# Delta-rule attention beside a mixture of experts: keys turned by VectorE and a staged copy, copies shared out anew

## What is computed

```
# gated delta rule, 16 key heads, 2 value heads per key head, D = 128
q, k, v, z = split(xn @ W_qkvz); b, a = split(xn @ W_ba)
q, k, v = silu(causal_conv4(q, k, v)); q, k normalised
beta = sigmoid(b); g = -exp(A_log) * softplus(a + dt_bias)
per chunk: M = -tril(k_beta k^T * decay, -1); T = (I - M)^-1
  v_new = T v_beta; k_cum = T (k_beta exp(g))
  vn = v_new - k_cum S;  out = (q exp(g)) S + tril(q k^T * decay) vn
  S = S exp(g_last) + (k exp(g_last - g))^T vn
attention = rmsnorm(out * silu(z)) @ W_out
# ffn: causal softmax attention (16 heads), then top-4 of 16 experts and a shared expert
```

## Time and profile before

| | us |
|---|---|
| median of three runs | 1550.68 |
| lowest, highest | 1547.57, 1552.07 |
| the profiled execution's own time | 1548.47 |
| its span, first to last instruction | 1546.7 |
| busy in it: PE, DVE, ACT, GpSimd | 98%, 71%, 50%, 29% |

### The profile page before, as it was taken

How to read it: one execution, slowest core, us unless ns; L and a number is a source line. 1 busy time by engine, 2 the same in 40 slices (tenths; PEclk the granted TensorE clock), 3 DMA queues, 4 the chain that set the end, 5 groups by cost and what they waited for, 6 DMA issues and landing times.

```text
span 1546.7 us, 29212 instructions
## 1 busy us (share of the span) xinstructions
PE 1514.5 (98%) x10946; PEld 1069.7 (69%) x10946; DVE 1104.5 (71%) x2452; ACT 779.7 (50%) x1680; POOL 442.7 (29%) x280
## 2 busy tenths in 40 slices
PE   6999999999999999999999999999999999999998
PEld 4666666767656776666767767767767668668667
DVE  5364544465366335698988988988888988988966
ACT  3444445344423334664564664664664565565552
POOL 1000000006024003354444444543442541541511
PEclk9999999999999999999999999999999999999999
DMA  4342433223144434324314414414313323223211
GB/s 135 99 150 96 156 124 109 66 64 125 54 128 130 124 109 120 94 51 97 100 35 107 107 32 108 105 36 106 78 50 91 70 60 86 69 66 86 60 22 35
DMA packets 225051, 136.88 MB, mean 89 GB/s; under 512 B 160976, under 2 KB 196304, under 8 KB 224912
## 3 DMA queue, kind: packets, MB, share of 16 engines
q1 hardware_dynamic: 221840, 126.62, 30.5%
q0 software_dynamic: 3072, 8.39, 1.8%
HBM read 94.85 MB, written 35.91 MB: 85 GB/s over the span
## 4 chain that ended last, share of the span: by engine, by line
PE 90%; DVE 3%; issue 2%; POOL 2%; ACT 1%; DMA 1%; SPq 0%; POOLq 0%; DVEq 0%; ACTq 0%
PE ps L953 7%; PE ps L814 7%; PE ps L575 7%; PE ps L835 6%; PE ps L670 5%; PE ps L600 4%; PE ps L1089 4%; PE ps L704 4%; PE ps L857 3%; PE ps L590 3%; PE ps L890 3%; PE ps L742 3%; PE ps L752 3%; PE ps L1112 3%; PE ps L867 3%; PE ps L889 2%
## 5 line engine op out<-in xcount | busy, mean ns | idle before, releaser
L1440 ACT ACTIVATE vs<-ps 128x256 f32<-128x256 f32 x128 | 49.2, 384 | 255.8 <-PE ps L857 251.6
L2389 POOL TENSOR_TENSOR qg<-qT,Ebc 128x1024 f32<-128x1024 f32 x32 | 74.7, 2354 | 354.4 <-PE ps L890 329.2
L1944 DVE SCALAR_TENSOR_TENSOR cv<-ps,cw,cv 128x1022 f32<-128x1022 f32 (+2 forms) x96 | 122.8, 1280 | 18.9 <-ACT cv L1380 14.9
L1955 DVE SCALAR_TENSOR_TENSOR cv<-ps,cw,cv 128x1022 f32<-128x1022 f32 (+2 forms) x96 | 122.6, 1277 | 4.0 <-ACT cv L1412 1.6
L835 PE MATMUL ps<-xnT,gz 128*128 128x512 f32 x256 | 121.0, 596 | 0.6 <-DVE cv L1944 0.6
L953 PE MATMUL ps<-wout,xT 128*128 128x256 f32 x480 | 120.2, 392 | 1.3 <-ACT vs L1427 0.9
L575 PE MATMUL ps<-xrT,cv 128*128 128x512 f32 x256 | 117.8, 593 | 1.1 <-ACT xrT L1277 0.8
L814 PE MATMUL ps<-xnT,gv 128*128 128x512 f32 x256 | 117.6, 603 | 0.5
L2083 DVE SCALAR_TENSOR_TENSOR total<-ps,rr,total 128x256 f32<-128x256 f32 x240 | 111.6, 481 | 5.7
L1340 ACT ACTIVATE we<-ps,bias 128x128 f32<-128x128 f32 (+3 forms) x128 | 65.8, 526 | 98.2 <-DVE bias L1764 98.2
L1760 DVE TENSOR_TENSOR ps<-ps,causal_neg 128x128 f32<-128x128 f32 x128 | 37.4, 292 | 105.2 <-PE ps L600 105.2
(11 more groups left out here) (265 smaller groups left out, 3567.9 us busy)
## 6 DMA issues: line engine op xcount, KB each, us to landing
xs_dram<-zeros SPq DMA_DIRECT2D x16, 1024.0 KB, 7.6
dec<-grow_dram SPq DMA_DIRECT2D x32, 512.0 KB, 4.7
Ebc<-erow_dram SPq DMA_DIRECT2D x32, 512.0 KB, 5.0
cv<-in_wqk SPq DMA_DIRECT2D x16, 512.0 KB, 3.6
xn<-xs_dram SPq DMA_DIRECT2D x47, 128.0 KB, 2.1
ys_dram<-yg SPq DMA_DIRECT2D x47, 128.0 KB, 2.0
we<-in_we SPq DMA_DIRECT2D x16, 352.0 KB
cv<-in_wv SPq DMA_DIRECT2D x16, 256.0 KB, 3.7
```

The costliest lines, as they stand in the source:

```text
L1944: ins = stt(row, pair(bank)[:, :, 0:S - k], cw[:, f, i, TAPS - 1 - k:TAPS - k], row, ALU.mult, ALU.add)
L1955: ins = stt(row, pair(bank)[:, :, 0:S - k], cw[:, n, 2 + r, TAPS - 1 - k:TAPS - k], row, ALU.mult, ALU.add)
```

## The change

1. **Keys.** `turn_keys(n)` leaves PE for n >= 1 (head 0 keeps it, ahead of the loop). DVE turns `kT` in blocks of 32 x 32 into T64c, which is free at that time; one instruction for 128 x 1024. The new `keys_across(n)` on SP puts the blocks where they belong across partitions: 16 SBUF-to-SBUF transfers of 32 rows by 1 KB into `sz[:, n % 2, 1]`, which `gate_silu(n,1)` writes only later. `decayed_keys` reads from there, both halves behind `deltas(h,2,b)`, and waits for these transfers and for MTc's, which count on one semaphore (`copies(n)`). GpSimd clears the part of T64c that must be zero (`empty_side`) afterwards.
2. **SP's order.** The copy into MTc is split off as `blocks_across` and stands behind `blocks_in` and `keys_across`.
3. **First states** are copied by ACT (`first_states`) between deltas 0 and deltas 1, instead of by DVE.
4. **Last merge:** ACT copies both halves of both steps.
5. **Experts:** DVE adds two tiles per head over 16 heads; GpSimd gathers four at the end of odd iterations.
6. PE's waits for the projections of keys and last values go from ACT's passes (`a_wk`) to DVE's `attention` products (`v_A`), the other readers of those banks. DVE's second `attention` product moves behind the residuals.

```diff
+        turned_keys = T64c[:].rearrange("p u c -> p (u c)").rearrange("p (j t c) -> p j t c", j=4, t=NT)
+        def staged_keys(n):
+            return sz[:, n % 2, 1].rearrange("p (i t c) -> p i t c", i=4, t=NT)
+        def copies(n):
+            return 64 + (64 + 256) * n
...
+            def keys_across(n):
+                if n >= 2:
+                    sp.wait_ge(fl["v_g"], 4 * (n - 1))
+                    sp.wait_ge(fl["a_wk"], 2 * (n - 1))
+                sp.wait_ge(fl["x_kt"], n + 1)
+                for i in range(4):
+                    for j in range(4):
+                        dma(staged_keys(n)[j * BL:(j + 1) * BL, i], turned_keys[i * BL:(i + 1) * BL, j])\
+                            .then_inc(fl["d_c"], 16)
...
                     blocks_out(n)
                     blocks_in(n)
+                    keys_across(n)
+                    blocks_across(n)
...
     # PE
                     if f >= 2:
-                        pe.wait_ge(fl["a_wk"], 2 * f)
+                        pe.wait_ge(fl["v_A"], 2 * f)
...
-                if middle:
-                    turn_keys(n)
...
     # ACT
+            def first_states(h, b):
+                act.wait_ge(fl["p_w"], 6 * h + b + 1)
+                if h:
+                    act.wait_ge(fl["p_o"], 8 * h)
+                fn(St[:, 1, b * R:(b + 1) * R, :].rearrange("p r d -> p (r d)"), ps[:, b, R * D:],
+                   ACT.Copy).then_inc(fl["x_S"], 1)
...
             def decayed_keys(n, r):
-                if r == 0:
-                    act.wait_ge(fl["p_kt"], n + 1)
-                    act.wait_ge(fl["v_cb"], n + 1)
-                    if n >= 2:
-                        act.wait_ge(fl["p_w"], 6 * (n - 1))
+                if n == 0:
+                    act.wait_ge(fl["x_kt"], 1)
+                else:
+                    act.wait_ge(fl["d_c"], copies(n))
...
                 for t in range(NT):
-                    last = fn(WT[:, n % 2, r, t, :], tiles(Y)[:, t, :], ACT.Copy, scale=cb[:, r, 1, t:t + 1])
+                    src = staged_keys(n)[:, :, t, :] if n else tiles(Y)[:, t, :].rearrange("p (i c) -> p i c", i=4)
+                    dst = WT[:, n % 2, r, t, :].rearrange("p (i c) -> p i c", i=4)
+                    last = fn(dst, src, ACT.Copy, scale=cb[:, r, 1, t:t + 1])
...
                 if middle:
                     gate_silu(n, 0)
-                    decayed_keys(n, 0)
                 if scan:
                     for b in range(B):
                         deltas(h, 2, b)
                 if middle:
-                    decayed_keys(n, 1)
+                    for r in range(R):
+                        decayed_keys(n, r)
...
     # DVE
+            def turn_keys(n):
+                dve.wait_ge(fl["p_u3"], 2 * n)
+                dve.transpose(turned_keys, kT[:, n % 2].rearrange("p t (j c) -> p j t c", j=4)).then_inc(fl["x_kt"], 1)
...
                 if middle:
-                    for r in range(R):
-                        attention(n, r)
+                    attention(n, 0)
+                if middle:
+                    turn_keys(n)
                 if scan:
                     for b in range(B):
-                        states(h, 0, b)
+                        residuals(h, 1, b)
+                if middle:
+                    attention(n, 1)
                 if scan:
-                    for b in range(B):
-                        residuals(h, 1, b)
+                    add_experts(h // 2, h % 2)
...
-                    beside_64(n)
                     add_outputs(h, 5, 7)
...
     # GpSimd
+            def empty_side(n):
+                pool.wait_ge(fl["d_c"], copies(n))
+                pool.memset(T64c[0:BL, :, BL:2 * BL], 0.0).then_inc(fl["g_zero"], 1)
```

More of the change, by code:

```diff
@@ L392, in blocks_out, with blocks_across @@
                     dma(mt_dram[q].rearrange("u p c -> p u c"), MT[rows, :, rows]).then_inc(fl["d_m"], 16)
+            def blocks_across(n):
                 if n:
@@ L477, in _ @@
                     blocks_in(0)
+                    blocks_across(0)
                 if s == SOLVE + SB + 4:
@@ L959, in first_blocks @@
                 pe.wait_ge(fl["d_t11"], 64 * (n + 1))
-                pe.wait_ge(fl["d_c"], 64 * (n + 1))
+                pe.wait_ge(fl["d_c"], copies(n))
                 if n:
@@ L1464, in gate_silu @@
                     act.wait_ge(fl["v_g"], 4 * (n - 1))
+                if n and r == 1:
+                    act.wait_ge(fl["a_wk"], 2 * n + 2)
                 fn(sz[:, n % 2, r].rearrange("p (b s) -> p b s", b=B), pair(gate_bank(n)), ACT.Silu).then_inc(fl["a_sz"], 1)
@@ L1589, in _ @@
                     for b in range(B):
+                        first_states(h, b)
+                    for b in range(B):
                         deltas(h, 1, b)
@@ L1609, in _ @@
                     take_key(f, 0)
+                if ahead:
                     silu_key(f)
@@ L2087, in add_outputs, with add_experts @@
                     ins.then_inc(fl["v_add"], 1)
-            def add_experts(i):
-                for a in range(4):
+            def add_experts(i, half):
+                for a in range(2 * half, 2 * half + 2):
                     t, j = i % 2 * 4 + a, i // 2
@@ L2233, in _ @@
                     system(n, 0)
-                if scan and middle:
-                    blocks_of_128(h)
                 if middle:
@@ L2240, in _ @@
                 if middle:
-                    for r in range(R):
-                        attention(n, r)
-                if scan:
-                    for b in range(B):
-                        states(h, 0, b)
+                    attention(n, 0)
+                if middle:
+                    turn_keys(n)
                 if scan:
@@ L2462, in _ @@
                 if middle:
+                    empty_side(n)
+                if middle:
                     if not ahead:
@@ L2476, in _ @@
                     key_norms(f)
-                if 0 <= n < 8:
-                    expert_rows(n)
+                if h % 2 and n // 2 < 8:
+                    expert_rows(n // 2)
 _OUT = (2, 512, 256)
```

84 lines of the change are left out of this document (38 added, 46 removed).

## The result

| | before | after |
|---|---|---|
| median (4 runs each), us | 1551.38 | 1624.55 |
| lowest, highest | 1547.57, 1552.42 | 1622.45, 1628.06 |
| the profiled execution: own time, span | 1548.47, 1546.7 | 1628.06, 1626.3 |
| mean granted clock of TensorE | 0.998 | 0.974 |

After over before is **1.0481** (95% interval 1.0465 to 1.0496): slower by 73 us, where I had forecast no change (1549.5) and had put the slow end of the range at 1585.

The account below looks back on a forecast made before the run. PE was taken as the bound. Net gain 0.45 us per head, less lateness: -2.9 (seven heads without gathers), +1.3 (seven with), +0.5 (head 14), total -1: 1547.4 profiled, 1549.5 median; range 1541 to 1585.

Parts of the forecast that it names:

- The path: Decayed keys come by DVE's transpose, 16 transfers and 16 ACT passes behind `deltas(h,2,b)`, with `deltas(h,3,b)` behind them.
- L: Landing of the last awaited transfer in h=9: 1186.7 or 1187.5 expected, no loss until 1187.9, gain gone at 1188.3.
- the view that shows the loss: PE's wait before `chunk_output(3)` and before the values was named as the loss to look for.
- the 16 issues: SP's key transfers per head, taken at 0.475 us a piece, 7.6 us in all, bounds 7.0 and 10.8.
- The last rival: SP is the bound: issues cost 0.634 + 0.04, L moves by 3.2, together +41 us: 1591; chance 0.20.
- the middle that I took: Start of `blocks_in` in heads with gathers, set at 1174.1, between 1173.3 and 1174.9.
- later by 1 us: Rival: SBUF passes at 0.3 instead of 0.25, or landing of 3.4, together +10 us: 1561; chance 0.15.
- wrong places of waits: Sign of error: PE waiting elsewhere, such as L843 (first states) or L1012 (copies that ACT took over).
- The returned wait: Between `solved(h,1,b)` and `new_state(h,1,b)`, 0.43 us comes back as PE's wait for ACT; net gain 0.45 per head.
- the prediction's first step: Eight transposes of `turn_keys` leave PE in 15 of 16 per-head groups, 0.88 us each, 13.2 us in all.
- VectorE's balance: Copies lost, one 128x1024 transpose gained at 1.35: -0.8 us per head, on an engine that is not the bound.
- The rule of the Trainium skill: Transposing 128x128 on TensorE if PSUM is acceptable: old form stays, the edit is worth 0 or less.

Follow-up runs that it names:

- e4: The changed kernel with the keys moved in 4 transfers of 128 rows per head instead of 16 of 32 (blocks in wrong partitions); ratio 0.9946.
- e2: The changed kernel plus 12 matmuls per head, results overwritten, in TensorE's queue ahead of `chunk_output(h,3)`; ratio 1.0331.
- e8: e1 with ScalarE's first eight passes of `decayed_keys` per head done twice, no transfer changed; ratio 1.0317.
- f1: e8 plus 12 matmuls per head that compute nothing, in TensorE's queue ahead of `chunk_output(h,3)`; ratio 1.0239.
- e3: The changed kernel with keys turned by TensorE as before, no key transfers, and point 6 of the change undone; ratio 1.0022.
- e5: e1 with ScalarE's prologue reordered: first U3s eviction behind `gate_silu(0,1)` and `decays(1,0)`, second behind `decays(1,1)`; ratio 1.0010.
- e1: The changed kernel with MTc's copies counted on their own semaphore, so ScalarE's passes wait for the 16 key transfers alone; ratio 1.0009.
- f3: f2 with one matmul of `project_gates(n,0,1)` moved between `solved(h,1,b)` and `new_state(h,1,b)`; ratio 0.9887, 1547.55 us.
- e6: e5 with 4 of the 16 key transfers issued by ScalarE, ahead of `gate_silu(n,0)`; ratio 1.0151.
- f2: e1 with the second U3s eviction behind the decays and 4 of the 16 key transfers issued by ScalarE behind `gate_silu(n,0)`; ratio 0.9910.

## Why the prediction was wrong

**The path was right, up to the issues.** PE bounds the kernel; the keys' path ends in `deltas(h,3,b)` and L decides. Offsets from the start of h=9, foreseen and measured: first store -0.37 and -0.47, `blocks_in` 3.1 and 3.06, the first transfer of keys 4.5 and 4.51. Foreseen was also the view that shows the loss, PE's wait before `chunk_output(3)`.

**The step that failed: "the 16 issues".** I took 0.475 us a piece, because plain transfers lay near 0.43 in the earlier trace rows, and 7.6 in all. They took 0.591 with a gap to the next, 0.63 to 0.74 a piece and 10.1 to 11.7 in all (10.67 in h=9). The row of 0.432 is a load from DRAM; the only SBUF-to-SBUF row there, 0.634, was the right one, and I set it aside for its short runs. e4 shows that the form of the data matters little (601 ns for four times as many rows). L came at 19.8 us in h=9, where the forecast had 16.5. The last rival had this price: its 3.2 us are 3.1 in h=9 (10.7 less 7.6), the rest of the difference is the tail of MTc's copies. I gave it a chance of 0.20. In even heads the store's landing was later as well, by 0.7 us on average against the middle that I took.

**A second term.** A pass that reads the staged keys in SBUF took 0.293 (4.69 to the squares' start for 16) where I had 0.25 from PSUM; the rival "later by 1 us" had named 0.3. Start of L to the deltas: 6.63, not 6.05. With 0.6 us times 15 heads this adds 9 us to the rival's 1591, and makes 1600.

**What was missing altogether: the clock behind idle time.** I priced each us of lateness at a us. About 1.8 us a head came on top (23 us in the 13 heads), from a granted clock of 0.5 to 0.6 behind the wait; e2, e8 and f1 show cause and size. In its loop the profile of before could not show it, since PE was never idle there. Ahead of the loop it did, twice: behind 2.27 us of idle time (to 413.93) and behind 2.97 us:

```profile
472.75 1.79 PE L769 MATMUL ps<-sqb,ones 128*32 128x512 f32 x8 [2.97 <-DVE MT L2162]
473.00:476.00 3.00, 3.00 (x15) 1.53 (x8) 3.00 (x1) 0.00 (x0) 3.00 (x1) 0.50 0.13 46
1209.57 1.04 PE L769 MATMUL ps<-sqb,ones 128*32 128x512 f32 x8
```

The granted clock is 0.50 there, and the eight matmuls of L769 take 1.72 us to the next start (474.47) where they take 0.97 (to 1210.54) in h=9. So the price of a wait of 2 to 3 us stood in the trace of before, and the mean clock of 0.998 hid it.

These parts add up to about the measured time (1591 + 9 + 23, and 3.5 for the next point, is 1627; measured 1624.6), but the rival's own 41 us rest on an average over heads, so the agreement is rough.

**Also missing: the prologue.** 3.5 us of the first head, slow clock included, come from the eviction that ScalarE took over, whose wait for PE now stands ahead of the exponentials (e3, e5). I had written only that wrong places of waits would be L843 or L1012. One eviction moved ahead of a gate in ScalarE's queue was enough. The first head's other 7.6 us (70.57 against e1's 62.97) are its 4.71 us ahead of L913 and the slow clock behind them.

**The returned wait** was taken as 0.43 of 0.88 a head, net 0.45. Measured: 0.59 net (e4 against e3), so 0.29 came back. Right in kind; f3 gets it back, for 0.89 in all, which is the 0.88 of the prediction's first step plus 0.06 of the other parts, less a rest of 0.05.

**Costed at nothing, rightly for the steady heads:** first states on ScalarE (ready in time in every variant), VectorE's balance (its transpose took 1.234 where I took 1.35), the experts' new order, GpSimd's memset: e3 holds all but the transpose and is within 0.1 us a head of before.

**The rule of the Trainium skill** (VectorE: DVE Perf Modes, "Rules for kernel authors": transpose 128x128 on TensorE) gave the right sign for the change as it was made, 1.0481, but not its reason. The transpose on VectorE hid in its slack; the path around it was late. With four issues less on SP and the shared counter undone the same transpose wins 1.1% with f3's moved matmul, so no run here bears the rule out as such.

## What to carry to other kernels

Before work is moved from the busiest engine to a queue of transfers, count the issues on the path and price them from a row of the same direction (SBUF to SBUF here), and let no wait include a transfer that its reader doesn't need: one shared counter was worth 4.7%. Where TensorE has never been idle, a wait of 2 to 5 us can cost more than itself, since the clock fell behind it in ten of the 13 steady heads of the changed kernel and in eight of e8's; ask for each new wait whether it may come at all, before asking how long it is. When a step is moved into an engine's idle time, look on which side of the instructions there the idle time lies: with four issues ahead of a gate a head took 60.13 us (e6), with the same four behind it 58.33 (f2).

## What the runs showed of the hardware

- The issue of a plain transfer from SBUF to SBUF on SP's queue takes 591 ns (median of 240) for 32 rows and 601 (of 60) for 128 rows, and the next starts 0.63 to 0.74 behind it (means over a head's 16); loads from DRAM took 432 in the earlier trace rows. On ScalarE's queue one lone issue took 0.51, and two with what lay between them 1.48.
- Behind 2 to 5 us of idle time TensorE's granted clock mostly fell to the lower level (0.50 and 0.57 in windows of 6 us). A head with the fall took 1.9 or about 3 us beyond its work and the wait, one without it 0.3; 13 heads of e8 had it 8 times. The same work with TensorE busy in place of idle ran at 1.00. Which waits are followed by it stays open.
- A 128x1024 fp32 transpose on VectorE takes 1.234 us, against 0.717 for 128x512.
- ScalarE's 128x128 passes come 0.293 us apart when they read the staged keys in SBUF (four runs of 32 elements), 0.25 apart when they read PSUM in one run. No run tells the memory from the runs.
